# A two-layer graph network: second-layer messages of 512 columns with the dot products in two parts

## What is computed

```python
hid = jax.nn.silu(edge_scalars @ fc_w1 * _inv(R))
w = hid @ fc_w2 * _inv(FC_HID)
w1, w2, w3, w4, w5 = jnp.split(w, [64, 128, 160, 192], axis=-1)
m_s1 = w1 * es * e0
m_s2 = w4 * jnp.einsum('eci,ei->ec', ev, e1) * _inv(3)
m_v1 = (w2 * es)[:, :, None] * e1[:, None, :]
m_v2 = w3[:, :, None] * ev * e0[:, :, None]
m_v3 = w5[:, :, None] * jnp.cross(ev, e1[:, None, :]) * _inv(2)
mid_s = jnp.concatenate([m_s1, m_s2], axis=-1)
mid_v = jnp.concatenate([m_v1, m_v2, m_v3], axis=1)
agg_s = jax.ops.segment_sum(mid_s, edge_dst, num_segments=n) * inv_nn
agg_v = jax.ops.segment_sum(mid_v, edge_dst, num_segments=n) * inv_nn
o_s = agg_s @ lin2_ws * a * _inv(S_MID)
o_v = jnp.einsum('nci,cd->ndi', agg_v, lin2_wv) * a[:, :, None] * _inv(V_MID)
```

## Time and profile before

| what | us |
|---|---|
| median of 3 runs | 3856.96 (3856.09 to 3858.71) |
| the profiled execution | 3859.59 |
| its span, from the first to the last instruction | 3858.0 |
| busy in the span: PE / DVE / ACT / POOL | 3505.2 / 3548.4 / 3054.7 / 2579.3 |
[...]

### The profile page before, as it was taken

One profiled execution on the slowest core, in us unless ns is written; L12 is line 12 of the kernel. 1 busy time (PEld: TensorE's weight loads), 2 busy tenths in 40 slices (PEclk: granted clock), 3 DMA queues, 4 the chain that ended last, 5 costly groups with the idle time before them and its releaser, 6 DMA issues. The chain is left out here.

```text
span 3858.0 us, 97024 instructions
## 1 busy us (share of the span) xinstructions
PE 3505.2 (91%) x21340; PEld 2634.3 (68%) x21340; DVE 3548.4 (92%) x12738; ACT 3054.7 (79%) x11217; POOL 2579.3 (67%) x2474
## 2 busy tenths in 40 slices
PE   4999999999999999999999976995999999999997
PEld 3888888888888888888888865884333333333335
DVE  5999999999999999999999997885999999999995
ACT  4888888888888888888888865774778777787774
POOL 1777777777777777777777720111777777777772
PEclk8999999999999999999999988997999999999999
DMA  4333333333333333333333338992343343334334
GB/s 110 92 94 95 94 92 91 92 91 91 91 91 92 91 90 91 93 91 91 91 91 92 91 113 260 274 254 83 91 95 93 95 96 92 95 95 96 93 95 116
DMA packets 296922, 411.00 MB, mean 107 GB/s; under 512 B 98581, under 2 KB 231573, under 8 KB 296597
## 3 DMA queue, kind: packets, MB, share of 16 engines
q0 software_dynamic: 127568, 211.04, 23.9%
q1 hardware_dynamic: 169284, 199.21, 16.0%
HBM read 309.09 MB, written 100.94 MB: 106 GB/s over the span
## 5 line engine op out<-in xcount | busy, mean ns | idle before, releaser
L657 POOL DMA_INDIRECT ACC<-src_tab,idx x784 | 817.4, 1043 | 330.8 <-issue 221.1
L657 POOL DMA_INDIRECT TAB<-dst_tab,idx x784 | 850.5, 1085 | 245.0 <-issue 152.1
L724 POOL DMA_INDIRECT ACC<-hid_tab,idx x784 | 810.8, 1034 | 245.7 <-issue 243.3
L803 PE MATMUL TR<-ident,M 128*128 128x128 f32 x4704 | 664.3, 277 | 86.6 <-DVE M L1535 73.8
L803 PEld LDWEIGHTS TR<-ident,M 128*128 128x128 f32 x4704 | 520.5, 141 | 180.0 <-DVE M L1535 177.5
L1129 ACT ACTIVATE MT<-TR 128x768 f32<-128x768 f32 x784 | 610.8, 862 | 3.5 <-PE TR L803 3.5
L1118 ACT ACTIVATE ACC<-W,ACC 128x64 f32<-128x64 f32 x2352 | 597.1, 360 | 0.0
L852 PE MATMUL HP<-w_hv,MT 128*128 128x128 f32 x3136 | 520.0, 288 | 0.0
L827 PE MATMUL E<-w_mv,MT 128*128 128x128 f32 x3136 | 477.1, 275 | 0.0
L827 PEld LDWEIGHTS E<-w_mv,MT 128*128 128x128 f32 x3136 | 437.0, 191 | 0.0
L1312 ACT ACTIVATE ACC<-TR,y 128x128 f32<-128x128 f32 (+1 forms) x1568 | 418.6, 553 | 11.4 <-PE TR L987 11.4
(11 more groups left out here) (279 smaller groups left out, 7828.3 us busy)
## 6 DMA issues: line engine op xcount, KB each, us to landing
h_tab<-ACC SPq DMA_DIRECT2D x392, 160.0 KB, 2.1
SC<-h_tab SPq DMA_DIRECT2D x50, 640.0 KB, 5.1
TAB<-h_tab SPq DMA_DIRECT2D x48, 640.0 KB, 5.2
ACC<-in_e64T SPq DMA_DIRECT2D x98, 256.0 KB
ACC<-src_tab,idx POOLq DMA_INDIRECT x784
TAB<-dst_tab,idx POOLq DMA_INDIRECT x784
ACC<-hid_tab,idx POOLq DMA_INDIRECT x784, 3.7
agg_tab<-ACC POOLq DMA_DIRECT2D x49, 240.0 KB, 4.1
```

The source lines that it names most:

```text
L657: pool.indirect_dma_start(tile[:, v.slot8, g, :], None, table.ap(), bass.IndirectOffsetOnAxis(ap=idx[:, v.sslot, c:c + 1], axis=0))\
L724: pool.indirect_dma_start(gat1[:, v.slot8, g, :], None, hid_tab.ap(), bass.IndirectOffsetOnAxis(ap=idx[:, v.sslot, c:c + 1], axis=0))\
L803: ins = nc.tensor.transpose(to[:, b * G + g, :], Mt[:, g, lo:lo + w], ident[:, :])
```

## The change

The message grows from 480 to 512 columns. L1857 now writes its three products for each channel into `M` itself, at columns 512, 480 and 448 (the stride is -32), and the tile gets 32 columns more, ML = 544, that hold the first of them and are not summed by PE. In place of the `tensor_reduce` a `tensor_tensor` adds columns 512 to 543 to columns 480 to 511: 32 columns for each of two groups, 64 in all. So each dot product stands in the message in two parts, columns 448 to 479 and 480 to 511, and `w_fi` has the 32 rows of `lin2_ws` for them twice. The cross products move from column 384 to 352. In the projection of the nodes the fourth transpose has 128 columns, ACT copies in one instruction instead of two, and the fourth matmul has 128 rows and 192 columns. There is one weight load (DMA) more at the start. The tiles `fA` and `fA2` go. No instruction changes its place on its engine.

```diff
-MW = 96 + 3 * 128
+MW = 128 + 3 * 128
+ML = MW + C
...
-        M = sb("M", [P, 2, G, MW])
+        M = sb("M", [P, 2, G, ML])
...
-        fA = sb("fA", [P, G, 3, C])
         fX = sb("fX", [P, G, 3, 2, C])
-        fA2 = sb("fA2", [P, G, 3, C])
...
-            load(w_fi[96:128, 2, 0:96], a["lin2_ws"][64:96, :])
+            load(w_fi[64:96, 3, 0:96], a["lin2_ws"][64:96, :])
+            load(w_fi[96:128, 3, 0:96], a["lin2_ws"][64:96, :])
...
-                load(w_fi[r, 3, 96 + i:96 + i + C], a["lin2_wv"][96:128, :])
+                rx = (96 + c) % P
+                load(w_fi[rx:rx + C, 2 + (96 + c) // P, 96 + i:96 + i + C], a["lin2_wv"][96:128, :])
...
-                    ins = nc.tensor.matmul(AG[v.sslot][:, 0:MW], ohE[:, v.slot, g, :], M[:, v.par, g, :],
+                    ins = nc.tensor.matmul(AG[v.sslot][:, 0:MW], ohE[:, v.slot, g, :], M[:, v.par, g, 0:MW],
...
-                for b, w in enumerate((P, P, P, 96)):
-                    ins = nc.tensor.transpose(turned[j % 4][0:w, b, :], ACC[:, j, P * b:P * b + w], ident[:, :])
+                for b in range(4):
+                    ins = nc.tensor.transpose(turned[j % 4][:, b, :], ACC[:, j, P * b:P * (b + 1)], ident[:, :])
...
-                nc.tensor.matmul(o[:, 96:192], tr[0:96, 3, :], w_fi[0:96, 3, 96:192], start=False, stop=True)\
+                nc.tensor.matmul(o[:, 0:192], tr[:, 3, :], w_fi[:, 3, :], start=False, stop=True)\
...
-                nc.scalar.activation(tr_n[0:96, j % 2, 3, :], turned[j % 4][0:96, 3, :], ACT.Copy)
-                nc.scalar.activation(tr_n[:, j % 2, 0:3].rearrange("p b e -> p (b e)"),
-                                     turned[j % 4][:, 0:3].rearrange("p b e -> p (b e)"), ACT.Copy).then_inc(s_fi["cp"], 1)
+                nc.scalar.activation(tr_n[:, j % 2].rearrange("p b e -> p (b e)"),
+                                     turned[j % 4].rearrange("p b e -> p (b e)"), ACT.Copy).then_inc(s_fi["cp"], 1)
...
-                dots = ch.count(TT(fA[:, :, :, :], feat(S, (C, 3), (1, C)), wgt(P + 64, (P, 3), (1, C)), ALU.mult))
+                dots = ch.count(TT(mid(MW, (-C, 3), (1, C)), feat(S, (C, 3), (1, C)), wgt(P + 64, (P, 3), (1, C)), ALU.mult))
...
-                nc.vector.tensor_reduce(Mt[:, :, 352:384], ax(fA[:, 0, 0, 0:1], (96, G), (1, C), (C, 3)), AX.X, ALU.add)
+                TT(mid(MW - C, (1, C)), mid(MW, (1, C)), mid(MW - C, (1, C)), ALU.add)
...
-                TT(mid(384, (C, 3), (1, C)), fX[:, :, :, 0, :], fX[:, :, :, 1, :], ALU.subtract)
+                TT(mid(352, (C, 3), (1, C)), fX[:, :, :, 0, :], fX[:, :, :, 1, :], ALU.subtract)
```

More of the change, by code:

```diff
@@ L1506, in mid @@
                 def mid(lo, *dims):
-                    return ax(Mt[:, 0, lo:lo + 1], (MW, G), *dims)
+                    return ax(Mt[:, 0, lo:lo + 1], (ML, G), *dims)
                 return mid, feat, wgt, ch.count(TT(mid(0, (C, 3), (1, C)), feat(S, (C, 3), (1, C)), wgt(160, (64, 3), (1, C)),
```

## The result

The changed kernel takes 3951.22 us (median of 5 runs, 3947.16 to 3953.91) where the kernel before takes 3857.31 (3856.09 to 3858.71) beside it: a ratio of 1.0243, 95% interval 1.0229 to 1.0257. It is 94 us slower, and outside the predicted range. The profiled execution had 3953.91, with a span of 3952.3.

The account below looks back on a forecast made before the run. Ring A was taken to bound the second layer at 22.45 us a super step, ring B close under it. Second layer -6.4, projection +2.0, transfers +0.3, extra load +0.5 gave -3.6 from 3856.96: 3853 us, range 3840 to 3867.

Parts of the forecast that it names:

- ring B: Second layer: path through PE and ACT from `fc` to `fc`; 21.58 us a super step, 22.20 after the change.
- ring A: Second layer: cycle of DVE's place 3 message, POOL's gathers and place 1's rows; sets the time, 22.45 us a super step.
- The sum, 0.93 + 8.12 + 5.82 + 7.67 = 22.54: Ring A's parts: place 6 gather's end, POOL's row, rows reaching DVE, DVE to place 3's message; taken as this super step.
- ring A becomes 21.7 to 22.0: Second layer: three faster DVE steps save 0.45 us a super step, POOL's stretch up to 0.3 more, from 22.45.
- The add's own cost: DVE, each step: the add costs 0.13 us where the reduce costs 0.28, a saving of 0.15.
- the add saves nothing: Rival: DVE's add waits for L1857's store and costs 0.28 us; ring A stays at 22.45, 3860 us; chance 0.08.
- ring B does not bind: Rival: PE takes the longer passes without later starts, ring A sets the time; 3823 to 3838 us; chance 0.12.
- the predicted floor of 22.20: Second layer: the super step cannot be shorter than ring B, however early DVE is; limits the gain to 12 us.
- Slower: the rings couple: Rival: through `M`'s two buffers late PE holds DVE on ring A; 22.62 us a super step, 3868 us; chance 0.15.
- The projection: Node projection on PE: fourth matmul 0.08 us longer in each of 25 tiles, +2.0 us; ACT's one copy taken as 0.

Follow-up runs that it names:

- e_narrow_add: Kernel before, 480 columns, with the reduce replaced by an add of two of the three products: 3955.27 us, ratio 1.0254.
- e_wide_reduce: Changed kernel, still 512 columns wide, with DVE summing the three products by tensor_reduce from fA again: 3872.42 us, ratio 1.0042.
- e_after_slow_dve: Changed kernel with a spare DVE add of 64 columns behind L1862 in each step: 4052.11 us, ratio 1.0502.
- e_after_memset: Changed kernel with L1862's add replaced by a memset of the same 64 columns, leaving out two products: 3859.54 us, ratio 1.0017.
- e_onehot_sbuf: Changed kernel with each step's one-hot (L1831) reading its row of numbers from SBUF instead of PSUM: 4050.54 us, ratio 1.0474.
- e_after_early_add: Changed kernel with the add and its wait moved up, straight behind the products it sums (L1857): 3855.44 us, ratio 1.0008.
- e_before_bubble: Kernel before with only DVE's wait for L1857's products moved up, straight behind L1857; the reduce stays in place: 3881.95 us, ratio 1.0066.
- e_before_much_pool: Kernel before with a spare POOL memset of 256 columns ahead of each step's two gathers: 3975.3 us, ratio 1.0311.
- e_before_far_wait: Kernel before with POOL's wait for DVE's message ahead of each step's gathers set back by four steps: 3852.20 us, ratio 1.0002.
- e_before_late_reduce: Kernel before with the reduce and its wait moved down by one operation, behind L1863: 4013.09 us, ratio 1.0418.
- e_before_early_reduce: Kernel before with the reduce and its wait moved up, straight behind L1857: 3876.64 us, ratio 1.0053.
- e_before_more_pool: Kernel before with a spare POOL memset of 8 columns ahead of each step's two gathers: 3855.04 us, ratio 1.0007.

## Why the prediction was wrong

POOL's row accounts for the second layer. It has hardly a gap but the 0.30 us ahead of each gather, so a super step is 16 x (mean gather + 0.30) + 1.02 for the adding DMA. The last column is the mean distance of the adding DMAs, the last one left out:

| kernel | mean gather, us | 16 x (mean + 0.30) + 1.02 | super step in the trace |
|---|---|---|---|
| before | 1.034 | 22.36 | 22.49 |
| after | 1.148 | 24.19 | 24.36 |
| e_narrow_add | 1.174 | 24.60 | 24.76 |
| e_wide_reduce | 1.044 | 22.52 | 22.65 |
| e_after_slow_dve | 1.285 | 26.38 | 26.45 |
| e_after_memset | 1.028 | 22.27 | 22.40 |
| e_onehot_sbuf | 1.272 | 26.17 | 26.39 |
| e_after_early_add | 1.022 | 22.17 | 22.29 |
| e_before_bubble | 1.059 | 22.76 | 22.91 |

The sum says only that POOL is never idle. That it sets the time, e_before_much_pool shows for the kernel before. In e_after_early_add POOL's row is full too, but so is PE's, as said under ring B.

- **The step that failed** is the reading of ring A: "The sum, 0.93 + 8.12 + 5.82 + 7.67 = 22.54, is this super step. Only three DVE steps lie on ring A". The sum proves nothing: its terms run from one message to the same message a super step on (3339.12 - 3316.58), and add up to a super step whatever lies between. The link that failed is the first. The 1.67 us of the gather at place 6 was put down to DVE's message at 3316.58, though the prediction itself noted that the row names no wait. But the one-hot starts at 3316.51, and the gather ends 1.00 after that:

```profile
3316.51 0.41 DVE L1831 TENSOR_TENSOR ohE<-E,dstf 128x256 f32<-128x256 f32 x1
```

  e_before_far_wait shows that the message doesn't hold the gathers, and e_onehot_sbuf that what DVE reads does. e_before_much_pool shows that POOL is on the path with all its gathers, not with seven.
- **"ring A becomes 21.7 to 22.0"** failed with it. The price of the edit was taken as time on DVE (0.15 us a step less). Its real price was on POOL, a term that the sum didn't have: the reduce was one of two breaks, and without it the mean gather went from 1.034 to 1.148 us, 16 x 0.114 = 1.8 us a super step, 89 in the layer.
- **The add's own cost** was right: the next operation starts 0.13 us later (3325.75 to 3325.88), and a step back to back has 2.49 us (3322.39 to 3324.88) for 2.63 before. So the rival "the add saves nothing" is out.
- **Ring B** was right in size. No two `fc` are closer than 11.11 us in the changed kernel, where none were closer than 10.79 before; 10.79 + 3 x 0.104 had it at 11.10. With no long gathers, in e_after_early_add, 81 of 96 distances lie within 0.05 of 11.11, PE is busy for 882 of the 900 us, and the super step is 22.29, beside the predicted floor of 22.20. So the rival "ring B does not bind", whose sign was halves of 10.8, is out, though in the changed kernel itself ring B mostly has slack (mean distance 12.3). The prediction let PE's weight loads speak for that rival, busy for 344 of the 900 us before, 38%. In e_after_early_add they are busy for 347, 39%, and the starts show that PE had no room there. PE's timeline of e_after_early_add:

```profile
3312.03 1.02 PE L978 MATMUL W<-ACC,fc 128*128 128x512 f32 x2
...
3323.14 1.02 PE L978 MATMUL W<-ACC,fc 128*128 128x512 f32 x2
```

- **"Slower: the rings couple"** had the sign (a super step over 22.5 and a longer wait for rows), but not the mechanism, and its 3868 was far too low. `M`'s buffers had no part in it: L1857 waited for PE 9.4 us in the window of 900.
- **The projection** costs more than the +0.08 a tile: the last matmul to the next tile's transpose takes 0.38 us (3938.95 to 3939.33) where the one of 96 columns took 0.25, 0.13 x 25 = 3.2 us for 2.0. ACT's one copy has a median of 597 ns where the two had 273 and 477, 0.15 us less in a tile. PE's timeline of the changed kernel:

```profile
3938.95 0.54 PE L1033 MATMUL W<-w_fi,MT 128*128 128x192 f32 x2
3939.33 0.60 PE L1021 MATMUL TR<-ident,ACC 128*128 128x128 f32 x4
```

Signs of it stood on the page of before: L724 the third costliest group, idle almost only for "issue". A view of who waits for whom has nobody to name for a queue that waits for nobody.

**What stays open.** Why the same break is worth so much at one place and so little at another. One reading is rhythm: a held gather that is let in at a break is done 0.91 later, and the next starts 0.30 after that, 1.21 in all. In the kernel before the breaks are 1.20 (one-hot to reduce) and 1.42 us apart, so each of a step's two gathers could find one:

```profile
3336.43 0.41 DVE L1831 TENSOR_TENSOR ohE<-E,dstf 128x256 f32<-128x256 f32 x1
...
3337.63 0.36 DVE L1862 TENSOR_REDUCE M<-fA 128x64 f32<-128x192 f32 x1
...
3339.05 0.41 DVE L1831 TENSOR_TENSOR ohE<-E,dstf 128x256 f32<-128x256 f32 x1
```

With the late reduce they are 1.8 and 0.82 apart, and in the changed kernel there is one a step. But e_before_early_reduce speaks against it: its breaks are 0.71 and 2.06 apart (the rows above), less even than those of the late reduce, and it takes 3877 us and not 4013. Nor do I know why a held gather is often let in between two operations with two sources: 158 gathers of e_after_early_add, and 86 of the changed kernel, none of them over 1.6 us, end 0.87 to 0.95 us after L1865's start. What a held gather depends on is shown by e_onehot_sbuf, where one source of DVE's moved into SBUF and 3951 us became 4051; what decides at which boundary the gather goes on is not shown. No version was found that beats the kernel before: PE's columns hold the wide messages at 22.2 us (2 x 11.11), and the narrow ones have POOL's row.

## What to carry to other kernels

Here DVE held up POOL's gathers without any semaphore between the two, by up to 5.7 us for one (6.60 where the shortest have 0.94). In another kernel with such gathers, look for POOL operations whose duration varies, and compare their ends with the starts of DVE's operations. Before a reduce, or an operation with a PSUM source, is replaced by one with two sources in SBUF, ask whether it is one of the few breaks in DVE's row. If it is, try a pause elsewhere: here one of 0.12 us at the step's start, made by moving one wait and one add, was worth 96 us (3951 to 3855), while a break moved by one operation cost 160 (e_before_late_reduce, 1.0418); which place is good has to be tried. An engine that stands idle only for "issue" may set the time: POOL did so at 78% busy (702 of 900 us), and more work on it told, with 120 us for a memset of 0.34 us a step (e_before_much_pool).

## What the hardware showed

- In these kernels indirect gathers issued by POOL (0.94 us at the shortest) sat through DVE operations with two sources in SBUF that ran back to back: one for 5.37 us, the longest for 6.60 (e_onehot_sbuf). Where DVE's row had an operation with one SBUF source, the gathers over 1.6 us ended about 0.92 us after its start (a one-hot with a source in PSUM: 74 of 74 in the changed kernel; a tensor_reduce: 119 of 119 in e_before_late_reduce, 0.91 us). With a memset in the add's place (e_after_memset, 3860 us), or a pause of 0.12 us at the step's start (e_after_early_add, 3855 us), none lasted over 1.6 us.
- A second SBUF source alone, in a one-hot that lasts 0.41 us either way, made 4051 us of 3951 (e_onehot_sbuf).
- The 0.30 us between POOL's operations had room for a small one: a memset of 8 columns in it (0.13 us) cost nothing that the times show (e_before_more_pool, 1.0007, 0.9997 to 1.0016).
